# Macaron block (MoE, causal attention, MoE) on one core: the attention stage rewritten in units of four heads

## What is computed

```python
x = x + 0.5 * _L0_ffn_ref(_layernorm(x, axis=-1), L0_ffn_Wg, L0_ffn_w1, L0_ffn_w2)
x = x + _L0_attn_ref(_layernorm(x, axis=-1), L0_attn_w_qkv, L0_attn_w_o)
x = x + 0.5 * _L0_ffn_ref(_layernorm(x, axis=-1), L0_ffn_Wg, L0_ffn_w1, L0_ffn_w2)
# inside _L0_attn_ref
qkv = jnp.einsum('bsh,oh->bso', hidden_states, w_qkv)
scores = jnp.einsum('bhqd,bhkd->bhqk', q, k) * scale
scores = jnp.where(causal, scores, jnp.finfo(scores.dtype).min)
probs = jax.nn.softmax(scores, axis=-1)
attn = jnp.einsum('bhqk,bhkd->bhqd', probs, v)
return jnp.einsum('bsh,oh->bso', attn, w_o)
```

## Time and profile before

| | us |
|---|---|
| median of 3 runs | 945.12 (944.35 to 1068.96) |
| profiled execution | 953.97 |
| its span, first to last instruction | 952.2 |
| TensorE busy | 809.7 (85%), 5820 matmuls |
| VectorE, ScalarE, GpSimd busy | 491.0, 411.6, 297.2 |

### The profile page before, as it was taken

How to read it: one execution, slowest core, us unless ns; L and a number is a source line. 1 busy time by engine, 2 the same in 40 slices (tenths; PEclk the granted TensorE clock), 3 DMA queues, 4 the chain that set the end, 5 groups by cost and what they waited for, 6 DMA issues and landing times. The chain is left out here.

```text
span 952.2 us, 16423 instructions
## 1 busy us (share of the span) xinstructions
PE 809.7 (85%) x5820; PEld 705.6 (74%) x5820; DVE 491.0 (52%) x1106; ACT 411.6 (43%) x743; POOL 297.2 (31%) x374
## 2 busy tenths in 40 slices
PE   4359999999998277999999999865369999999995
PEld 2149999999998265776677677533159999999995
DVE  7744534454441576655765765615924543445440
ACT  3114534455342232665465465444024453445531
POOL 1063455444333400211111211110163445544233
PEclk9659999999999569999999999998569999999998
DMA  9143354424421400100201100106054235442311
GB/s 332 24 129 100 88 139 126 121 50 118 110 24 23 155 1 2 45 2 17 75 1 45 45 0 1 46 1 199 3 174 111 75 93 140 122 115 57 95 23 22
DMA packets 56682, 72.62 MB, mean 76 GB/s; under 512 B 10400, under 2 KB 48288, under 8 KB 56608
## 3 DMA queue, kind: packets, MB, share of 16 engines
q1 hardware_dynamic: 41280, 52.84, 16.8%
q0 software_dynamic: 15360, 19.23, 11.0%
HBM read 53.82 MB, written 19.01 MB: 76 GB/s over the span
## 5 line engine op out<-in xcount | busy, mean ns | idle before, releaser
L974 ACT ACTIVATE at_probs<-at_ps_keys 128x896 f32<-128x896 f32 (+1 forms) x128 | 96.0, 759 | 83.2 <-PE at_ps_keys L1263 74.0
L539 DVE SCALAR_TENSOR_TENSOR first_h_lo<-first_ps_h,first_h_hi 128x320 fp32r<-128x320 f32 x128 | 61.4, 491 | 114.0 <-ACT first_h_hi L408 107.5
L539 DVE SCALAR_TENSOR_TENSOR second_h_lo<-second_ps_h,second_h_hi 128x320 fp32r<-128x320 f32 x128 | 61.4, 491 | 113.6 <-ACT second_h_hi L408 108.1
L332 POOL DMA_INDIRECT out_dram<-second_scaled,second_add_now x40 | 69.2, 1731 | 123.2 <-ACT second_scaled L401 119.8
L332 POOL DMA_INDIRECT after_first<-first_scaled,first_add_now x40 | 68.8, 1720 | 123.4 <-ACT first_scaled L401 118.6
L634 PE MATMUL first_ps_o<-first_w_hi,first_h_hi 128*128 128x256 f32 x320 | 91.3, 285 | 0.0
L634 PE MATMUL second_ps_o<-second_w_hi,second_h_hi 128*128 128x256 f32 x320 | 91.1, 285 | 0.0
L634 PE MATMUL first_ps_o<-first_w_hi,first_h_lo 128*128 128x256 f32 x320 | 90.1, 282 | 0.0
L634 PE MATMUL first_ps_o<-first_w_lo,first_h_hi 128*128 128x256 f32 x320 | 90.1, 282 | 0.0
L634 PE MATMUL second_ps_o<-second_w_hi,second_h_lo 128*128 128x256 f32 x320 | 90.0, 281 | 0.0
L634 PE MATMUL second_ps_o<-second_w_lo,second_h_hi 128*128 128x256 f32 x320 | 90.0, 281 | 0.0
(11 more groups left out here) (256 smaller groups left out, 1996.7 us busy)
## 6 DMA issues: line engine op xcount, KB each, us to landing
first_w_raw<-in_L_ffn_w_dram SPq DMA_DIRECT2D x16, 1024.0 KB
second_w_raw<-in_L_ffn_w_dram SPq DMA_DIRECT2D x16, 1024.0 KB
at_xt<-at_xt_all SPq DMA_DIRECT2D x3, 1024.0 KB, 5.0
x<-_attn_hidden_states_dram SPq DMA_DIRECT2D x4, 512.0 KB, 5.5
normed_rows<-first_xn SPq DMA_DIRECT2D x4, 512.0 KB, 7.5
x<-after_first SPq DMA_DIRECT2D x4, 512.0 KB, 7.4
at_x_now<-after_first SPq DMA_DIRECT2D x4, 512.0 KB, 4.8
out_dram<-x SPq DMA_DIRECT2D x4, 512.0 KB, 3.2
```

Source lines behind the costliest of these rows:

```text
L332: pool.indirect_dma_start(sum_rows, bass.IndirectOffsetOnAxis(ap=add_now[par][:, s:s + 1], axis=0), scaled[par][:, s, :], None, bounds_che ...
L539: v.scalar_tensor_tensor(h_lo[:, f, a * HALF:(a + 1) * HALF], ps_h[:, f % 2, a, 0:HALF], 0.0, h_hi[:, f, a * HALF:(a + 1) * HALF].bitcast( ...
L974: act.activation(probs[h // GROUP][:, h % GROUP, columns], keys_columns(half), ACT.Exp, scale=float(HD) ** -0.5).then_inc(exped, 1)
```

## The change

In the first stage's prologue:

- `AttentionWeights` holds the attention's weights for the whole kernel. Ten DMAs load them on SyncE's queue after the normalized rows are stored; TensorE turns the 16 blocks after the two products of positions and before the 32 list products; ScalarE writes `hi`; VectorE writes `lo` after the lists are done.
- The mask tables become `pick`, `hide_half`, `hide_half_t`: 64 rows each in two halves, made of 12 `affine_select` instead of 2.

In the attention stage:

- A unit is 4 heads of one batch (16 units); two units share a tile of stacks, of which three are kept (`STACKS = 3`).
- `stacks(f)` projects with the weights as the stationary side, so q and k come out transposed, 12 products of 512 columns for a tile. The row stack, its turns and GpSimd's copies go. Twelve DMAs of 128 KB copy `hi` and `lo` into the rows of `q_stack` and `k_stack`.
- Row scores and key scores run over 48 or 50 rows (0 to 49 or 64 to 113) instead of 128: one product for the even and one for the odd head of a pair, into two banks. `k_stack` holds no zeros. Row scores cover exactly the causal columns, as key scores do (128 to 512), where before the least was 256.
- One item of row scores is one or two pairs followed by four mask products of 64 rows that mask all of its heads. Key scores have no masks.
- `PLAN` is one list for all engines. Step v holds the key scores of unit v, the row scores of unit v+2, the turned maxima of unit v+1, the values of unit v-1, the turned outputs of unit v-2, and one piece of the front of a later batch (rows, stacks, values). Everything is unrolled.
- PSUM is two slots of two banks for front items and two for keys and values; an item waits until the one two before it in its list is read.
- Normalization of batches 1 to 3 moves to GpSimd (`pow` and multiplications), and `x` is kept, so that it isn't loaded a second time.

```diff
-    UNIT_HEADS = HEADS // 2
-    BESIDE = [[("turn", 0)], [("project", 2)], [("turn", 1)], [("project", 3), 0, 1], [("turn", 2), 2, 3], [4, 5],
-              [("turn", 3), 6, 7], [8, 9], [10, 11, 12], [13, 14], [15, 16, 17], [18, 19], [20, 21], [22, 23], [], []]
+    UNITS = BATCH * HEADS // GROUP
+    STACKS = 3
+    KEY_STEPS = [(0,), (1,), (2, 3)]
...
+        if v < -1:
+            return normal + work + sum(S, [])
+        return (normal + S[0] + N[0] + S[1] + N[1] + turns + N[2] + S[2] + N[3] + S[3] + work + outputs + S[4] + N[4] + S[5] +
+                N[5] + project)
...
+            def stacks(f):
...
+                sp.wait_ge(hi_done, HI_AT[item] + 1)
+                for to, slots, which in ((q_stack, (0, 1), 0), (k_stack, (0, 2), 1)):
+                    for slot in slots:
+                        for odd in range(2):
+                            row = odd * STACK + slot * HD
+                            sp.dma_start(to[f % STACKS][row:row + HD, :, :].bitcast(F32),
+                                         pre_hi[odd * STACK:(odd + 1) * STACK, which, :].bitcast(F32)).then_inc(stack_in, 16)
...
+            def stacks(f):
+                hh = f % 2
+                banks = claim_front(("stacks", f))
+                pe.wait_ge(front_v, FRONT_V[FRONT_AT[("rows", f // 2)]])
+                for which in range(2):
+                    for k in range(DK):
+                        hi, lo = (w[:, 8 * k + 2 * which + hh, :] for w in (w_hi, w_lo))
+                        last = three(banks[:, which, :], (hi, xt[:, 0, k, :]), (hi, xt[:, 1, k, :]), (lo, xt[:, 0, k, :]),
+                                     first=(k == 0), end=(k == DK - 1))
...
+            def scores(v, n):
+                qt, keys, pairs = score_shape(n)
+                f = v // 2
+                if n == 0:
+                    pe.wait_ge(stack_in, 16 * STACK_DMAS * (f + 1))
+                banks = claim_front(("scores", v, n))
+                for i, p in enumerate(pairs):
+                    a = 2 * (v % 2) + p
+                    for odd in range(2):
+                        rows = slice(odd * STACK, odd * STACK + BOTH)
+                        pe.matmul(banks[:, odd, i * keys:(i + 1) * keys], q_stack[f % STACKS][rows, a, qt * P:(qt + 1) * P],
+                                  k_stack[f % STACKS][rows, a, 0:keys], start=(i == 0), stop=False)
                 for part in range(2):
...
+                    for odd in range(2):
+                        rows = slice(odd * STACK, (odd + 1) * STACK)
+                        blocks = banks[:, odd, 0:len(pairs) * keys].rearrange("p (a c) -> p a c", c=keys)[:, :, qt * P:]
+                        last = pe.matmul(blocks, const.pick[rows, part, :],
+                                         const.hide_half[rows, part, :].unsqueeze(1).broadcast_to([STACK, len(pairs), P]),
+                                         start=False, stop=(part == 1))
...
-            def key_scores(b, hh, i):
...
+            def keys(v, p, j):
+                item = ("keys", v, p, j)
+                f, a = v // 2, 2 * (v % 2) + p
...
+                for kt in KEY_STEPS[j]:
+                    for odd in range(2):
+                        rows = slice(odd * STACK, odd * STACK + MAX_ROW + 2)
+                        last = pe.matmul(banks[:, odd, at:at + SEQ - kt * P], k_stack[f % STACKS][rows, a, kt * P:(kt + 1) * P],
+                                         q_stack[f % STACKS][rows, a, kt * P:SEQ], start=True, stop=True)
...
```

More of the change, by code:

```diff
@@ new lines, in head_turn @@
+    def head_turn(v):
+        if v >= PER_BATCH and v % 2 == 0:
+            b, k = (v - PER_BATCH) // PER_BATCH, v % PER_BATCH // 2
+            return (b, k) if v < UNITS else None
+        return None
+    PLAN = [("normalize", 0)]
+    for v in range(FIRST, UNITS):
+        PLAN += step_plan(v)
+    last = BATCH - 1
+    PLAN += [("turns", None, (last, 0)), ("outputs", UNITS - 1, UNITS - 2), ("outputs", None, UNITS - 1),
+             ("turns", None, (last, 1)), ("project", last)]
+    FRONT_USERS = ("rows", "values_in", "stacks", "scores", "turns", "project")
@@ new lines, in attention, with by_scalar, by_vector @@
+    FRONT = [item for item in PLAN if item[0] in FRONT_USERS]
+    KEYS = [item for item in PLAN if item[0] in ("keys", "outputs")]
+    def by_scalar(item):
+        what = item[0]
+        return what in ("values_in", "keys") or (what in ("turns", "outputs") and item[1] is not None)
+    def by_vector(item):
+        what = item[0]
+        return what in ("rows", "stacks", "scores", "project") or (what in ("turns", "outputs") and item[2] is not None
+                                                                               and item[2] != -1)
@@ new lines, in counted @@
+    def counted(users, by):
+        return list(itertools.accumulate(int(by(item)) for item in users))
+    FRONT_A, FRONT_V = counted(FRONT, by_scalar), counted(FRONT, by_vector)
+    KEYS_A, KEYS_V = counted(KEYS, by_scalar), counted(KEYS, by_vector)
+    HI = [item for item in PLAN if item[0] in ("rows", "stacks") or (item[0] == "turns" and item[2] is not None)]
+    FRONT_AT = {item: n for n, item in enumerate(FRONT)}
+    KEYS_AT = {item: n for n, item in enumerate(KEYS)}
+    HI_AT = {item: n for n, item in enumerate(HI)}
@@ L733, in attention @@
+    TURNS_OF = {item[1]: item for item in FRONT if item[0] == "turns" and item[1] is not None}
+    OUTPUTS_OF = {item[1]: item for item in KEYS if item[0] == "outputs" and item[1] is not None}
+    STACK_DMAS, MAX_DMAS = 12, 2
     with ExitStack() as stack:
@@ L874, in _ @@
-            sp.sem_inc(max_in, 64)
-            load_x(FIRST)
-            insert_max(FIRST, 0)
-            sp.wait_ge(early_kept, 12)
-            load_xt(1)
-            insert_max(FIRST, 1)
-            with sp.Fori(1, LAST) as b:
-                batch(b, True)
-            batch(LAST, False)
-            store(LAST)
+                sp.dma_start(row_tiles(out_rows, QT * b, QT), x[:, QT * b:QT * (b + 1), :]).then_inc(rows_stored, 16)
+            for v in range(FIRST, UNITS):
+                if 0 <= v + 1 < UNITS:
+                    insert_max(v + 1)
+                for item in batch_work(v):
+                    if item[0] == "stacks":
+                        stacks(item[1])
+                if v >= 8 and v % PER_BATCH == 0:
+                    store(v // PER_BATCH - 2)
@@ L1206, in project @@
                 for k in range(DK):
-                    tiles = slice((2 * k + hh) * 3, (2 * k + hh + 1) * 3)
-                    hi, lo = (w[:, tiles, :].rearrange("p a c -> p (a c)") for w in (w_hi, w_lo))
-                    last = three(out, (xt[:, 0, k, at], hi), (xt[:, 0, k, at], lo), (xt[:, 1, k, at], hi),
-                                 first=(k == 0), end=(k == DK - 1))
+                    for j in range(QT):
+                        last = pe.transpose(banks[:, k, j * P:(j + 1) * P], xn[:, j, k * P:(k + 1) * P], const.identity[:])
@@ L1346, in finish @@
-            def finish(b):
-                all_values(b, 1)
-                turn_o(b, 1, 1)
-                for part, n in PROJECTION[1:]:
-                    part(b, n)
-            unit_loop(pe, front, step, finish)
+                last.then_inc(front_made, 1)
+            pe.wait_ge(const.ready, 1)
+            for item in PLAN:
+                what, of = item[0], item[1:]
+                if what != "normalize":
+                    {"rows": rows, "stacks": stacks, "values_in": values_in, "scores": scores, "turns": turns,
+                     "keys": keys, "outputs": outputs, "project": project}[what](*of)
```

881 lines of the change are left out of this document (380 added, 501 removed).

## The result

The changed kernel has a median of 906.6 us (902.9 to 911.8, 4 runs) against 946.0 before (944.4 to 947.0, and one slow run of 1069 that is left out of the comparison): a ratio of 0.959, 95% interval 0.955 to 0.964. So it is faster by 39 us, where 83 were forecast; 906.6 stands just outside the range of 836 to 906. The profiled execution took 903.75 us, with a span of 901.8. That of before lay 8 us above its own median, and its two feed-forward stages were 11.6 us longer than those after with the same code, so I compare the attention stage alone: from 316.0 to 646.2 before (330.2 us), from 309.3 to 600.7 after (291.4). The 38.8 less match the 39.4 between the medians.

The account below looks back on a forecast made before the run. TensorE's instruction stream was taken to bound the attention stage's middle, dependent steps its beginning. 17.6 us from the beginning and 65 from units and end made 83 less: 953.97 to 871, or 862 as median, range 836 to 906.

Parts of the forecast that it names:

- part 1: Attention units: TensorE's work for 4 heads, 12.7 us with 5%, makes 13.0 a step with waits, against 17.0.
- the rival of row halves in turn: Rival in attention steps, chance 0.16: a pair's products run one after the other, step 15.6 us, 900 in all.
- full pairing: Rival in attention steps, chance 0.10: even and odd heads run fully side by side, 11.5 us a step, 840 in all.
- 0.3 for waits at the slots: Attention steps: TensorE's allowance for waiting at the slots, 0.3 us within the 13.0 us step.
- engines in lockstep: Rival in attention steps, chance 0.12: late-freed slots hold up TensorE's fixed order, 1.6 us a step, 888 in all.
- low clock: Rival in attention units, chance 0.05: waits keep TensorE's clock low, some 190 us of work takes 150 more, 1012.
- part 5: Attention from first key scores to its end: steps of 13.0, 10.5 and 6.7 us, end 15; 203 together, 65 less.
- Part 4: Attention stage's beginning: a chain of dependent steps brings the first key scores near 360, 17.6 us earlier (10 to 25).
- 128 KB need about 0.6 and the issue sets the pace: Stack copies on SyncE's queue: 0.71 us to issue each, so 16 DMAs take 11.4 us in two steps of 26.
- Part 3: SyncE's queue in attention units: stack copies and maxima, 11.4 us of issue in two steps of 26, both hidden.
- Part 6: First stage's prologue: added weight turns, low parts and selects fit into idle time, cost 0 (0 to +3) us.
- Part 2: Attention steps: VectorE's 9.6 us and ScalarE's 7.7 stay below TensorE's 13.0, so neither takes over.

Follow-up runs that it names:

- order_spread: Changed kernel with row and key scores alternating, and turned maxima, batch work and values product together at a step's end; 887.7 us, ratio 0.937 to the kernel before.
- one_row_group: Changed kernel with both products of a pair and all masks on the even head's rows, so one after the other; 952.0 us, ratio 1.003 to the kernel before.
- Half maxima: Changed kernel with VectorE taking each row maximum over the first half of the keys only; 876.9 us, ratio 0.928 to the kernel before.
- warm_start: Changed kernel with idle TensorE products added before the first key scores, during the copy wait and after early row-score items; 911.3 us, ratio 0.965 to the kernel before.

## Why the prediction was wrong, step by step

- **Direction and size.** Faster was right. Of the 83 us, 39 came.
- **TensorE's work, the sum of part 1: right in kind, 1.0 too high.** 12.7 us for four heads were counted, the 5% with it; the steps 5 to 10 of order_spread, all at clock 1.00, have 11.5 to 12.2 busy, 11.7 in the mean. Pairs run side by side, so the rival of row halves in turn falls; its price was 38 us, and one_row_group shows 42 to 45. The rule of the Trainium skill on row groups, which part 1 weighed ("TensorE: Matmul & The Clock Gate", Part 3), agrees with the starts 0.03 us apart. The row scores took 2.3 us, nearer to the 2.6 of *full pairing* than to the 3.6 taken, so the 1.0 added for filling and changes of type was not there. The drain at a change of tiling mode ("TensorEngine Tiling (Array Packing)", Key Properties, of the Trainium skill) shows in no row as a cost of its own.
- **The step that failed: "0.3 for waits at the slots".** TensorE mostly waits for VectorE, a sign that the prediction named for being wrong. In the step shown the waits are 2.56 us of 14.10. For the eleven steps the forecast held 139.7 us of work and 3.3 of waits; measured are 134.89 busy and 26.5 idle: 23.2 more of waits, 4.8 less of work. The error in the work hid part of the error in the waits, and the 13.1 us steps of order_spread, with 11.6 to 11.9 busy, meet the forecast 13.0 partly by luck. My ground was that VectorE has three quarters load. That is a mean; the load comes in a burst of four maxima of up to 1.17 us against 0.5 to 0.9 us of products for each. The rival *engines in lockstep* had the mechanism, priced at 1.6 a step and given 0.12. Half maxima (30 us less) and the spread order (19 less, same work, same mean clock in the eleven steps) show it. How much of the 19 belongs to the parted burst and how much to the later turned maxima isn't known.
- **The clock, "an engine as full as before".** Steps 0 to 10 took 161.4 us (366.24 to 527.63), 14.7 each, 18 us above 143. From step 4 on, a step at clock 1.00 took 13.3 to 14.2, and one at 0.81 to 0.89 took 15.7 to 17.9. The *low clock* rival holds in this mild form: 0.95 in the middle, 0.72 at 381 to 405. The masks show that the clock can move the time (920.5 with 0.78 in the middle, 899.0 with 1.00). But it is not what the better orders won back: their eleven steps have the same 0.89.
- **The end of part 5.** From 527.63 to the stage's end 73.0 us against 59.9. The three steps without front work took 12.8, 12.1 and 9.1, 33.9 against 31.5. The next step took 12.2 against 6.7, at a mean clock of 0.72: its 32 products with the values alone took 4.50 us, where they take 2.36 at the full clock. The last step and the end took 26.9 against 21.7, at 0.86. Both have waits for ScalarE's exponentials and for divided outputs too; no experiment was made on them alone.
- **Part 4, the beginning: 4.6 us earlier, not 17.6.** Counted from the stage's start, the last copy was issued at 29.3 us (28.2 forecast), landed at 36.3 (29.5), and the first key scores came 20.7 later (14.5). "128 KB need about 0.6 and the issue sets the pace" failed: twelve copies of 128 KB take 14.7 us from first issue to landing, 107 GB/s, 1.2 us each, twice what the earlier trace rows gave for one copy of 1024 KB. In the 20.7 us TensorE is busy 15.5, all of it at clock 0.50, and waits for halves and maxima; a high clock ahead of them changed nothing, and none of my runs had one through the whole of them. Part 4 had priced the turns and the first tile at the low clock, but had no term for it here. GpSimd's `pow` took 1.05, not 0.5.
- **Part 3, "both are hidden": right**, since a whole step lies between, though the copies' price was not. From 346 us on TensorE has no wait for `stack_in` or `max_in` in the changed kernel. The margin is thinner than thought: with projections at a step's end the copies are late by up to 2.9 us, and with two stacks they cost 74.
- **Part 6: right.** The list products stand at their old times, first expert product at 63.90 against 64.08.
- **Part 2: right in the sum** (VectorE 9.09 busy in 14.10, ScalarE 7.63; 9.6 and 7.7 forecast), and misleading as an argument: a sum over the step does not tell the waits within it.

By the medians 45 us are missing. In the profiled stage the beginning accounts for 13.0, steps 0 to 10 for 18.4 and the rest for 13.1, together 44.5. So the waits in the steps are the largest single error, 23.2 us of them, but not the whole: 6.8 us more went by until the copies had landed, 6.2 more from there to the first key scores, and 13.1 more in the last steps and the end. What makes the clock fall while TensorE never stops is open.

## What to carry to other kernels

Where two engines pass blocks through a few slots in a fixed order, add up each run of neighbouring items and not only the whole step: an engine with 65% load held the other up where its items stood together. Another order of the same work gave 19 us, halving that engine's longest work 30. So spread the items that a second engine must answer between the long ones that it doesn't. And price a transfer from one of its own shape: a copy of 1024 KB told little of twelve of 128 KB into 16 partitions each.

## What the runs showed of the hardware

- In these runs busy time does not tell the granted clock: 104.10 of 125 us busy at 0.78 without masks, 103.51 at 0.95 with them, 109.01 at 1.00 with twice as many. With all pairs in one row group, products one after the other with no gap in the profile went from 1.00 to 0.50 among those of 48 and 50 rows, and the values product came with 1.00 again. In warm_start TensorE was busy 12.00 of 12 us from 353 to 365 us at 0.50.
- Added products on an engine that waits made a kernel faster (8 us here) and removed ones slower (14 us).
- Two products of 512 columns in two halves of the rows start 0.03 us apart, and such a pair with its four masks takes 0.43 us where one product with one mask took 0.36.
- Twelve copies between on-chip buffers, 128 KB into 16 partitions each, took 14.7 us from first issue to landing (107 GB/s); from 333 to 345 us they moved 117 GB/s at a DMA share of 0.96, with two issuing queues 125 at 1.02. Whether their size or their shape makes them slower than one copy of 1024 KB was not tried.
